# The last stage of a vision tower: expert results added into the output by accumulating scatters

## The reference, cut to what matters

```python
h = h + _L1_attn_ref(_layernorm(h), ...)      # the second attention
h = h + _L1_ffn_ref(_layernorm(h), ...)       # the token experts, below

logits = flat @ Wr                            # 8192 tokens, 8 experts
top_vals, top_idx = jax.lax.top_k(logits, 2)
top_w = jax.nn.softmax(top_vals, axis=-1)
gates = zeros.at[arange(N)[:, None], top_idx].add(top_w)
for e in range(E):
    hdn = gelu(flat @ W1[e] + b1[e])
    y = hdn @ W2[e] + b2[e]
    out = out + gates[:, e:e + 1] * y
```

## Time and profile before

| What | Value |
|---|---|
| median of 3 timed runs | 1534.49 us (1532.92 to 1535.9) |
| the profiled execution's own time | 1528.62 us |
| its span in the trace | 1526.8 us |
| busy in the span: PE, ACT, DVE, POOL | 1202.5, 993.9, 928.9, 578.6 us |
| second attention | about 925 to 1162 us |
| planning | 1172 to 1196 us |
| token experts | 1196 to 1480 us |
| adding the results | 1483 to 1526.8 us |

### The profile page before, as it was taken

One profiled execution on the slowest core, in us unless ns is written; L12 is line 12 of the kernel. 1 busy time (PEld: TensorE's weight loads), 2 busy tenths in 40 slices (PEclk: granted clock), 3 DMA queues, 4 the chain that ended last, 5 costly groups with the idle time before them and its releaser, 6 DMA issues. The chain is left out here.

```text
span 1526.8 us, 26947 instructions
## 1 busy us (share of the span) xinstructions
PE 1202.5 (79%) x9465; PEld 804.9 (53%) x9465; DVE 928.9 (61%) x2492; ACT 993.9 (65%) x1348; POOL 578.6 (38%) x548
## 2 busy tenths in 40 slices
PE   3698898989898989915999994789871399999930
PEld 2344343434343434404788883677761288888820
DVE  5365868687768785541666665787752166666622
ACT  0487687868786869900989993454520399999920
POOL 3422333333333332230000001167775257777654
PEclk9599999999999999957999997788865599999975
DMA  3472737272727272212222200011111566777619
GB/s 94 95 186 70 165 91 168 87 169 86 170 86 170 82 169 83 84 29 73 94 79 88 83 28 11 1 35 45 48 46 47 216 222 233 233 242 246 230 52 300
DMA packets 108920, 180.88 MB, mean 118 GB/s; under 512 B 15867, under 2 KB 80854, under 8 KB 101742
## 3 DMA queue, kind: packets, MB, share of 16 engines
q1 hardware_dynamic: 81166, 129.62, 30.8%
q0 software_dynamic: 17344, 42.68, 8.3%
q10 hardware_dynamic: 10272, 6.82, 1.9%
HBM read 117.27 MB, written 63.12 MB: 118 GB/s over the span
## 5 line engine op out<-in xcount | busy, mean ns | idle before, releaser
L445 ACT ACTIVATE a_probs<-a_psS 128x1024 f32<-128x1024 f32 x512 | 483.1, 1042 | 119.2 <-PE a_psS L530 62.7
L964 DVE TENSOR_TENSOR f_g_lo<-f_g,f_g_hi 128x512 fp32r<-128x512 f32 x284 | 195.7, 690 | 162.4 <-ACT f_g L875 159.9
L542 PE MATMUL a_psO<-a_probs,a_v 128*32 128x256 f32 x4096 | 284.7, 397 | 0.3 <-ACT a_probs L445 0.3
L872 ACT ACTIVATE f_g_hi<-f_psH,f_w 128x512 fp32r<-128x512 f32 x284 | 198.8, 700 | 40.2 <-PE f_psH L71 38.0
L1757 POOL DMA_INDIRECT result<-f_out,f_idx x156 | 182.7, 1171 | 102.4 <-issue 60.0
L530 PE MATMUL a_psS<-a_qs,a_ks 50*128 50x512 f32 x1024 | 192.8, 455 | 19.2 <-ACT a_probs L445 9.7
L875 ACT ACTIVATE f_g<-f_psH,f_w 128x512 f32<-128x512 f32 x284 | 198.7, 700 | 0.0
L542 PEld LDWEIGHTS a_psO<-a_probs,a_v 128*32 128x32 f32 x4096 | 109.1, 111 | 137.0 <-issue 91.4
L530 PEld LDWEIGHTS a_psS<-a_qs,a_ks 50*128 50x128 f32 x1024 | 78.9, 190 | 121.0 <-ACT a_probs L445 67.5
L69 PE MATMUL f_psH<-f_x_hi,f_w 128*128 128x512 f32 x284 | 124.5, 438 | 5.1 <-DMA f_w<-experts 4.2
L1267 POOL DMA_INDIRECT queue<-all_row,all_idx x112 | 109.5, 978 | 32.9 <-issue 32.7
(11 more groups left out here) (294 smaller groups left out, 2120.7 us busy)
## 6 DMA issues: line engine op xcount, KB each, us to landing
f_w<-experts SPq DMA_DIRECT2D x55, 1026.5 KB, 5.3
experts<-a_split POOLq DMA_DIRECT2D x32, 512.0 KB, 4.4
f_rows<-queue SPq DMA_DIRECT2D x39, 260.0 KB, 5.3
qparts<-a_parts SPq DMA_DIRECT2D x16, 512.0 KB, 4.4
a_qs<-qparts SPq DMA_DIRECT2D x32, 256.0 KB, 4.8
kparts<-a_parts SPq DMA_DIRECT2D x14, 512.0 KB, 3.4
a_ks<-kparts SPq DMA_DIRECT2D x28, 256.0 KB, 6.7
a_qs<-qparts SPq DMA_DIRECT2D x32, 128.0 KB, 5.7
```

The lines of the kernel that those rows point to most:

```text
L445: nc.scalar.activation(probs[u % NPR][:, :], psS[score_buffer(u)][:, :, :].rearrange("p a n -> p (a n)"), ACT.Exp).then_inc(exp_done, 1)
L542: last = nc.tensor.matmul(psO[32 * g:32 * g + 32, a * HALF:(a + 1) * HALF], v[par][:, 2 * hp + p, kt, :], probs[u % NPR][:, cols:cols + HA ...
L872: nc.scalar.activation(g_hi[i][:, n, :], psH[n][:, :], ACT.Gelu, bias=bias(m, n))
L964: nc.vector.tensor_tensor(g_lo[i][:, n, :], g[:, n, :], g_hi[i][:, n, :].bitcast(F32), ALU.subtract).then_inc(lo_done, 1)
```

## The change

Three things change together.

```diff
-def block_attention(nc, H, queue, counts, row, idx, sent, ident, half, ins, B, S, D):
+def block_attention(nc, H, out, out_in, queue, counts, row, idx, sent, ident, half, ins, B, S, D):
...
+            for b in range(B):
+                sp.wait_ge(h_done, (b + 1) * 2)
+                sp.dma_start(out[b * S:(b + 1) * S, :].rearrange("(t p) d -> p t d", p=P), H[:, b * T:(b + 1) * T, :]).then_inc(out_in, 16)
...
+                nc.vector.tensor_tensor(new_e[:, 1:N], e_f[:, 1:N], e_f[:, 0:N - 1], ALU.is_equal)
+                dve.drain()
+                nc.vector.scalar_tensor_tensor(new_e[:, 1:N], new_e[:, 1:N], -16.0 * TPC, whole[:, 1:N], ALU.mult, ALU.add)
+                dve.drain()
+                nc.vector.tensor_copy(tile_after[:, 1:N], new_e[:, 1:N])
...
         @block.gpsimd
         def _(pool):
+            pool.wait_ge(total_in, B * 16)
+            after = {m: pool.value_load(tile_after[0:1, m:m + 1], min_val=16 * TPC, max_val=(m + 1) // 2 * 16 * TPC) for m in range(3, N)}
             for m in range(N):
                 i = m % 2
                 pool.wait_ge(out_ready, m + 1)
+                if m > 2:
+                    pool.wait_ge(sent[1 - i], after[m])
+                elif m:
+                    pool.wait_ge(sent[1 - i], (m + 1) // 2 * 16 * TPC)
                 for j in range(TPC):
-                    pool.indirect_dma_start(result, bass.IndirectOffsetOnAxis(ap=idx[i][:, j:j + 1], axis=0), out[i][:, j, :], None,
-                                            bounds_check=2 * B * S - 1, oob_is_err=False).then_inc(sent[i], 16)
+                    pool.indirect_dma_start(total, bass.IndirectOffsetOnAxis(ap=idx[i][:, j:j + 1], axis=0), out[i][:, j, :], None,
+                                            bounds_check=B * S - 1, oob_is_err=False, compute_op=ALU.add).then_inc(sent[i], 16)
...
-def add_results(nc, H, result, out, B, S, D):
...
-    a["place_of"] = (np.arange(128)[:, None, None] + np.arange(K)[:, None] * b * S + np.arange(b * S // 128) * 128).astype(np.int32)
+    a["place_of"] = (np.arange(128)[:, None, None] + np.zeros((K, 1), int) + np.arange(b * S // 128) * 128).astype(np.int32)
```

More of the change, by code:

```diff
@@ L1613, in _, with plan_tiles @@
             route(B - 1)
-def plan_tiles(nc, queue, counts, row, idx, sent, tile_e, tile_row, ins, E, B, S, D):
+def plan_tiles(nc, queue, counts, row, idx, sent, tile_e, tile_row, tile_after, ins, E, B, S, D):
     STRIDE = B * S + CH
@@ L1629, in plan_tiles @@
         over, part = c.sb("over", [1, N, E]), c.sb("part", [1, N, E])
-        e_f, done_f, row_f = (c.sb(n, [1, N]) for n in ("e_f", "done_f", "row_f"))
+        e_f, done_f, row_f, new_e, whole = (c.sb(n, [1, N]) for n in ("e_f", "done_f", "row_f", "new_e", "whole"))
         steps, number = c.sb("steps", [1, 1, M]), c.sb("number", [1, N])
@@ L1638, in _ @@
             def _(sp):
[L1639 removed]
+                for dst, n in ((upto[:, :, :], "upto"), (steps[:, :, :], "steps"), (number[:, :], "number"), (whole[:, :], "whole"), (pad_place[:, :, :], "pad_place")):
                     sp.dma_start(dst, ins[n]).then_inc(tab_in, 16)
@@ L1701, in _, with token_experts @@
                 dve.sem_inc(done, 1)
-def token_experts(nc, queue, result, tile_e, tile_row, ident, parts, ins, B, S, D):
+def token_experts(nc, queue, total, total_in, tile_after, tile_e, tile_row, ident, parts, ins, B, S, D):
     E, _, WIDE = parts.shape
@@ L1783, in token_experts @@
                      x_ps, t_ps, y_done, NB, D)
-def add_results(nc, H, result, out, B, S, D):
[L1788 to L1819, removed]
-                for b in range(B):
-                    dve.wait_ge(both, b + 1)
-                    h = H[:, b * T:(b + 1) * T, :]
-                    nc.vector.tensor_tensor(h, h, y[b][0][:, :, :], ALU.add).then_inc(summed, 1)
 def tower(nc, ins, out):
@@ L1854, in tower @@
         tiles = K * B * S // CH + E - 1
-        tile_e, tile_row = c.sb("tile_e", [1, tiles], I32), c.sb("tile_row", [1, tiles], I32)
+        tile_e, tile_row, tile_after = (c.sb(n, [1, tiles], I32) for n in ("tile_e", "tile_row", "tile_after"))
+        out_in = c.sem("out_in")
         queue = nc.dram_tensor("queue", [E * (B * S + CH) + CH, ROW], F32).ap()
-        result = nc.dram_tensor("result", [K * B * S, D], F32).ap()
         row = [c.sb(f"row{p}", [P, K, S // P, ROW]) for p in range(3)]
@@ L1860, in tower @@
         sent = [c.sem(f"sent{p}") for p in range(3)]
-        block_attention(nc, H, queue, counts, row, idx, sent, ident, half, ins, B, S, D)
-        plan_tiles(nc, queue, counts, row, idx, sent, tile_e, tile_row, ins, E, B, S, D)
-        token_experts(nc, queue, result, tile_e, tile_row, ident, experts[1], ins, B, S, D)
-        add_results(nc, H, result, out, B, S, D)
+        block_attention(nc, H, out, out_in, queue, counts, row, idx, sent, ident, half, ins, B, S, D)
+        plan_tiles(nc, queue, counts, row, idx, sent, tile_e, tile_row, tile_after, ins, E, B, S, D)
+        token_experts(nc, queue, out, out_in, tile_after, tile_e, tile_row, ident, experts[1], ins, B, S, D)
 def host(inputs):
@@ L1904, in host @@
     a["number"] = np.arange(N).astype(np.float32)[None]
-    a["pad_place"] = np.tile((K * b * S + np.arange(128)).astype(np.int32)[:, None, None], (1, 4, 1))
+    a["whole"] = ((np.arange(N) + 1) // 2 * 16 * 4).astype(np.float32)[None]
+    a["pad_place"] = np.tile((b * S + np.arange(128)).astype(np.int32)[:, None, None], (1, 4, 1))
     T = S // 128
```

2 lines of the change are left out of this document (1 added, 1 removed).

## The result

The changed kernel takes 1570.89 us (median of 4 runs, 1569.89 to 1575.47) against 1533.70 for the kernel before (4 runs): a ratio of 1.0248, 95% interval 1.0222 to 1.0274. It is 37 us slower. 1501 us was forecast, with a range up to 1542. The profiled execution took 1569.89 us, its span is 1568.1.

The account below looks back on a forecast made before the run. PE was taken to bound the kernel at 6.45 us per tile, with POOL becoming the bound at 6.77. Gain 46.6 from the removed tail, less 13.5, is 33 us: 1534.5 to 1501 us, range 1486 to 1542.

Parts of the forecast that it names:

- The bound before: Experts' stage: PE sets the pace at 6.45 us per tile, POOL close behind with its own need of 5.56.
- The tail removed: End of the kernel: without the last block the span ends near 1480.2 instead of 1526.8, a gain of 46.6 us.
- The early stores: Second attention: eight 512 KB stores of the stream from SP cost 0.
- Planning and register loads: Before the experts: three more planning operations (0.8 us, covered) and 36 register loads on POOL (25 us, hidden) cost 0.
- A scatter that accumulates, e: Experts' stage: extra POOL time of one accumulating scatter, four per tile, taken as 0.1 us.
- the high end: Extra POOL time per accumulating scatter of 0.46 us, if every place is worked out twice.
- The low end: Extra POOL time per accumulating scatter possibly nothing, since direct copies of 512 KB and 16 KB cost 607 and 514 ns.
- The order waits: Experts' stage: nine waits for the tile just issued hold POOL 3.5 us each, 0.81 us per tile over 39 tiles.
- the first rival: Experts' stage: accumulating costs POOL almost nothing, landings near 2.0 us, PE still paces; 1488 to 1492 us, chance 0.20.
- the second one: Experts' stage: POOL's extra time on 156 scatters takes the gain back, slower beyond 0.31 us each; chance of slower 0.13.
- Third: Experts' stage: accumulates fill the DMA engines at 3.4 times a copy's cost; chance 0.07, shared with long landings.
- Fourth: Experts' stage: order waits hold POOL at every tile, 117 us more, 1605 us; chance 0.02, shared with late loads.

Follow-up runs that it names:

- e11: Changed kernel, results to separate scratch rows, no order waits or register loads, two of a tile's four scatters accumulating: 1542.61 us, ratio 0.974 to the kernel before.
- e13: Changed kernel, results to separate scratch rows, no order waits or register loads, three of a tile's four scatters accumulating: 1565.25 us, ratio 0.988 to the kernel before.
- e14: Changed kernel, results to separate scratch rows, no order waits or register loads, all four scatters accumulating: 1588.74 us, ratio 1.003 to the kernel before.
- e10: Changed kernel, scatters as plain copies to separate scratch rows, no order waits, register loads or last block: 1542.31 us, ratio 0.972 to the kernel before.
- e5: Changed kernel, scatters replaced by direct POOL copies to fixed scratch rows, no order waits or register loads: 1537.58 us against 1582.15 for the kernel before.
- e7: Kernel before plus the eight early stores in the second attention, its last block storing again: 1585.13 us, ratio 1.0024.
- e6: Changed kernel, scatters replaced by direct accumulating POOL DMAs to fixed scratch rows, no order waits or register loads: 1537.51 us against 1582.15 for the kernel before.
- e1: Changed kernel with scatters that copy instead of adding, order waits and all else kept: 1568.90 us, ratio 0.9907 to the kernel before.
- e16: Changed kernel, four accumulating scatters to separate scratch rows, no order waits or register loads, only 64 of 128 rows sent per scatter: 1563.71 us.
- e15: Changed kernel, four accumulating scatters to separate scratch rows, no order waits or register loads, only half of each row's bytes sent: 1584.35 us.
- e4: Changed kernel loading weights for the first four tiles only, later tiles reusing them: 1604.01 us, ratio 1.0131 to the kernel before.

## Why the prediction was wrong, by its own steps

- **The bound before**: right. PE at 6.45 us per tile, POOL's own need at 5.56. The threshold worked out from these two decided e11, e13 and e14 within 5 us.
- **The tail removed**: right in kind, a little large. 46.6 less one for the accumulate's landing was forecast, 43.4 came in the trace; alone it is worth 41 (e10) to 45 us (e5).
- **The early stores**: 0 forecast. SP's padding starts 4.9 us later than before and POOL's last send 4.0 later, so some 4 us were lost by the end of the attention. But 2.6 of them are there when SP loads that block's tables, ahead of every early store, as these rows of the kernel before and of the changed one show:

```profile
929.09 0.64 SPq L1252 DMA_DIRECT2D a_before<-before  x1
```
```profile
931.71 0.83 SPq L1252 DMA_DIRECT2D a_before<-before  x1
```

  At most 1.4 us are left for the stores in these traces; e7 shows no cost either.
- **Planning and register loads**: right. Of the three operations 4.9 - 4.0 = 0.9 us show on SP (0.8 forecast). The first scatter's idle time of 39.07 us was ended by DVE, so the 36 loads were hidden.
- **A scatter that accumulates, e**: this is the step that failed. The mechanism, POOL as the bound, came as forecast; this term of the sum was far too small. I took 0.1 and set the high end at 0.46; measured is 1.55 against 0.98 unhindered, 0.57, and 0.50 in the rhythm of a POOL that never pauses. The mean of 1593 ns is above the 1.5 us that the prediction had named as the sign of being wrong. The high end came from what an indirect DMA costs over a direct one. That was the wrong neighbour: e5 and e6 show the accumulate as a price of its own, 0.35 us where no place is looked up. The low end, from two direct copies of different size, said nothing on it either. With 0.50 the prediction's own formula gives 5.56 + 2.00 + 0.81 = 8.37 us per tile, 75 us lost, and 1534.5 - 45.6 + 75 = 1564 us, against 1570.89 measured; the 4.8 us of the later start and the 2.2 that the tail gave less make up the rest.
- **The order waits**: the total was right by luck, since errors in its parts cancel. 9 x 3.5 = 31.6 us were forecast; the trace has 30.9 in eight gaps and 2.83 in a ninth that DVE ended. But no landing is near 3.0. The gaps are 5.1 to 5.8 us beside weight loads and 2.1 to 2.4 otherwise. With the 0.74 us taken off that lie between DVE's go (1260.67) and POOL's start (1261.41) they give landings of some 4.4 to 5.0 and 1.3 to 1.6 us, an estimate. The averaging over 39 tiles holds once POOL is the bound. Under PE's pace it would have made the waits free, and in e1 they were not. By e1's ratio of 0.9907 the first rival (e = 0) would have come to about 1520 us in place of 1488; since e1 ran only in a group at 1583 us, where other holds were passed on too, this is an estimate and not shown.
- **The rivals**: the second one, POOL takes all back by e, happened, with e beyond its upper end. It had 0.13 of the chance, and the range left it out above 1542; an unseen operation on the engine with 0.34 us to spare deserved more. Third: it did not bind, the DMA share is 0.71 over the first 200 us and 0.59 after. But it was nearer than the prediction had it. With its 0.21 us for a copy, 0.37 more is 2.8 times a copy, against 3.4 at which the engines are full; with PE at its pace e6 has a share of 0.98. Fourth: refuted, a landing held POOL eight times.
- **The Trainium skill's pages**: the Trainium skill, "DMA: Bandwidth & Descriptors", Anatomy of one DMA, lets one expect no incremental cost here; where page and measurement differ, the measurement decides. The accumulate costs POOL 0.57 us more per scatter, of which at most 0.28 go with the 128 rows and their packets (e16) and none with the bytes (e15). As to the box on DVE blocking SWDGE DMAs in the Trainium skill, "SBUF — State Buffer", and the two figures that the section behind it gives: the accumulating scatters range from 1.543 to 2.047 us with a mean of 1.593, so even if all of the stretch is DVE's doing, it adds 0.05 us on average. The trace does not show the factor of five.

## What to carry to other kernels

Before an operation that no trace shows is put on an engine, compare that engine's spare time per item with the spread of its possible price: here 0.34 us in the rhythm of the rows and 0.9 at POOL's own pace, against 4 x 0.57 us. Below the threshold the same operation costs little or nothing. A wait that holds an engine for several items' slack is not to be taken as free because the average fits: in e1 23 us of such waits came through in the stage, though the engine had time on average, and in other traces a single one was absorbed. And a block that waits for its loads gets shorter with their bytes, by 10 us here, until the next engine binds, and hardly with fewer or larger transfers.

## What was not expected of the hardware

- An accumulating DMA from SBUF goes out as one packet per row of 512 bytes (128 packets) where the copy needs 16; POOL's time goes from 0.98 to 1.55 us (indirect) and from 0.53 to 0.88 (direct). It depends little on the rows (1.41 us for 64) and not on their width.
- The same accumulates keep the DMA engines busier: a share of 0.98 in place of 0.75 for the same 246 GB/s (e6, e5).
- POOL's wait for the landing of a scatter, 2.1 to 2.4 us at best, is 5.1 to 5.8 us beside 1 MB weight loads, and as long for a copy (up to 6.02, e1) as for an accumulate. Without the loads it is 3.4 at most (e4).
- The same kernel on the same chip took 1583 us in one group of runs and 1532 in another, 3% apart, with narrow spread in each. Only ratios within a group are safe.
